# Normalizing on the eviction of spatial products taken by columns, full spectral products, high modes first, packed bias rows, scores without GpSimd

## The reference

```python
x = x + codano(group_norm(x))            # layer 0
t = t + attention(layer_norm(t)); t = t + experts(layer_norm(t))   # layer 1
# in codano, tn = instance_norm of each of 128 token images
k, q = fno_layer(tn, key...), fno_layer(tn, query...)    # to 64 x 64, 16 heads
v = fno_layer(tn, value...)                              # 128 x 128, 16 heads
p = softmax(q.k / scale)                                 # 32 x 32 for each head and batch
attn = fno_layer(p.v, proj...)                           # back to one channel
# fno_layer(x) = (conv1x1(x) + bias) + irfft(rfft(x)[low modes] * w)
```

## Time and profile before

| | us |
|---|---|
| runs of before, median of 3 (lowest, highest) | 2422.3 (2421.1, 2422.91) |
| the profiled execution, its own time | 2420.67 |
| its span | 2418.6 |
| stages tokens, modes, scores, mix (from the start of the span) | to 93.2, 123.2, 151.7, 248.8 |
| busy over the span: PE, DVE, ACT, POOL | 2090.5, 1936.0, 1710.9, 627.7 |

### The profile page before, as it was taken

One profiled execution on the slowest core, in us unless ns is written; L12 is line 12 of the kernel. 1 busy time (PEld: TensorE's weight loads), 2 busy tenths in 40 slices (PEclk: granted clock), 3 DMA queues, 4 the chain that ended last, 5 costly groups with the idle time before them and its releaser, 6 DMA issues. The chain is left out here.

```text
span 2418.6 us, 31035 instructions
## 1 busy us (share of the span) xinstructions
PE 2090.5 (86%) x10467; PEld 1065.6 (44%) x10467; DVE 1936.0 (80%) x3563; ACT 1710.9 (71%) x2429; POOL 627.7 (26%) x761
## 2 busy tenths in 40 slices
PE   8667548957499999999999999999999999766778
PEld 8522225743254444444444444444444444323333
DVE  4766888868788898898898888888888888767776
ACT  1454436639287888888888888888888888657776
POOL 0345403506501021022022022022000000036778
PEclk9888655556699999999999999999999999878999
DMA  9002443000000000000000000000000000000111
GB/s 301 1 35 105 114 108 76 1 0 1 6 1 1 1 1 1 1 1 1 1 1 1 1 1 1 1 1 1 1 1 1 1 1 1 9 14 23 31 32 44
DMA packets 80833, 55.72 MB, mean 23 GB/s; under 512 B 11283, under 2 KB 78739, under 8 KB 79140
## 3 DMA queue, kind: packets, MB, share of 16 engines
q1 hardware_dynamic: 75476, 52.38, 7.3%
q10 hardware_dynamic: 5200, 1.38, 0.3%
HBM read 36.90 MB, written 16.78 MB: 22 GB/s over the span
## 5 line engine op out<-in xcount | busy, mean ns | idle before, releaser
L1909 ACT ACTIVATE inner<-banks,key_bias,scales 128x1024 f32<-128x1024 f32 x512 | 616.9, 1205 | 211.6 <-PE banks L1782 205.9
L2031 DVE TENSOR_TENSOR weights_low<-weights,weights_high 128x1024 f16<-128x1024 f32 x512 | 674.7, 1318 | 17.0
L1916 ACT ACTIVATE weights<-inner 128x1024 f32<-128x1024 f32 x512 | 541.0, 1057 | 16.3 <-DVE weights_low L2031 0.3
L2027 DVE CAST weights_high<-weights 128x1024 f16<-128x1024 f32 x512 | 371.0, 725 | 181.5 <-ACT weights L1916 167.6
L2105 POOL CAST sums_high<-sums 128x512 f16<-128x512 f32 x32 | 39.1, 1222 | 1092.9 <-ACT sums L1899 1075.0
L1782 PE MATMUL banks<-queries_high,keys_high 128*128 128x512 f16 x1024 | 304.8, 379 | 0.7 <-ACT inner L1909 0.7
L1797 PE MATMUL banks<-weights_low,tokens_high 128*128 128x512 f16 x1024 | 304.8, 379 | 0.0
L1782 PE MATMUL banks<-queries_low,keys_high 128*128 128x512 f16 x1024 | 304.7, 379 | 0.0
L1797 PE MATMUL banks<-weights_high,tokens_low 128*128 128x512 f16 x1024 | 304.7, 379 | 0.0
L1797 PE MATMUL banks<-weights_high,tokens_high 128*128 128x512 f16 x1024 | 304.7, 379 | 0.0
L1782 PE MATMUL banks<-queries_high,keys_low 128*128 128x512 f16 x1024 | 304.7, 379 | 0.0
(11 more groups left out here) (592 smaller groups left out, 3373.7 us busy)
## 6 DMA issues: line engine op xcount, KB each, us to landing
images_b<-in_x SPq DMA_DIRECT2D x32, 256.0 KB, 9.1
images_a<-in_x SPq DMA_DIRECT2D x8, 1024.0 KB, 9.2
mixed_scratch<-images_a SPq DMA_DIRECT2D x4, 2048.0 KB, 6.3
result<-group_result SPq DMA_DIRECT2D x32, 256.0 KB, 2.3
images_b<-mixed_scratch SPq DMA_DIRECT2D x10, 768.0 KB, 5.1
...
```

The source lines that it names most:

```text
L1909: act.activation(m.inner[:, t % 2, :], m.pair[t % 2], ACT.Exp, scale=m.fs[:, 1:2], bias=m.kb[:, c // QN % 2, k:k + 1]).then_inc(s.inner, 1)
L1916: act.activation(m.wt[:, t % 2, :], m.inner[:, t % 2, :], ACT.Exp).then_inc(s.outer, 1)
L2027: vec.tensor_copy(m.wH[:, t % DEEP, :], m.wt[:, t % 2, :]).then_inc(s.high, 1)
L2031: vec.tensor_tensor(m.wL[:, t % DEEP, :], m.wt[:, t % 2, :], m.wH[:, t % DEEP, :], ALU.subtract)\
```

## The change

- Tokens: the parameters' transfers are issued first; VectorE makes the effective weights between the second and third quarter of its statistics; TensorE turns them and ScalarE evicts them ahead of the second transform; the averaging matmuls move from groups 29 and 31 to 26 and 28; a part of the statistics moves into the loop of low parts; there are five chunks.
- Modes: `m.hg` comes first on VectorE and TensorE, the low modes behind it; bias terms become three more rows (36 to 38) of the group `few`, by three further columns of the table `low`.
- Scores: VectorE makes j = 0, 1, 4 and half of the heads of 2, ScalarE the other half and 3; the eight bias matmuls are gone.
- Normalizing images_a in place is gone in three stages. A spatial product now takes the four columns of one group, so that its eviction can apply that group's scale and offset; the offset needs the row sums of the mixing matrix, one matmul and one VectorE instruction. `m.probT` is one full block-diagonal matrix, so that a spectral product is one matmul over 128 partitions, in a ring of three pairs of banks. All four stores wait for the last eviction.

```diff
 def stage_tokens(nc, held, m, ins, const):
-    chunks = [(0, 6), (6, 18), (18, 42), (42, 66)]
+    chunks = [(0, 6), (6, 18), (18, 36), (36, 54), (54, 66)]
...
-                    if g < len(SCALARS):
-                        scalar(g)
-                    elif g < len(SCALARS) + len(convs):
-                        conv(g - len(SCALARS))
-                    if g == 31:
+                    if g < len(convs):
+                        conv(g)
+                    elif g < len(convs) + len(SCALARS):
+                        scalar(g - len(convs))
+                    if g == 29:
                         act.wait_ge(s.added, 1)
+            act.wait_ge(s.wturned, 1)
+            act.copy(m.wT[:, 0:4].rearrange("p k c h -> p (k c h)"), m.ps[2])
+            act.copy(m.wT[0:MT[4][1], 4].rearrange("p c h -> p (c h)"), m.ps[3][0:MT[4][1], 0:128])
+            act.copy(m.wq[:, 0].rearrange("p c h -> p (c h)"), m.ps[3][:, 128:256])
+            act.copy(m.wq[0:FEW, 1].rearrange("p c h -> p (c h)"), m.ps[3][0:FEW, 256:384]).then_inc(s.wcopied, 1)
             act.wait_ge(s.fixed, 1)
...
-                if g == 29:
+                if g == 26:
...
-                if g == 31:
+                if g == 28:
...
-            pe.wait_ge(s.split, 3)
+            pe.wait_ge(s.split, 7)
+            pe.wait_ge(s.wready, 1)
+            pe.wait_ge(s.copied, NG)
+            for k, (m0, n) in enumerate(MT):
+                for cpt in (0, 1):
+                    o = m.ps[2][0:n, 64 * (2 * k + cpt):64 * (2 * k + cpt) + 64] if k < 4 else m.ps[3][0:n, 64 * cpt:64 * cpt + 64]
+                    pe.transpose(o, m.weff[:, cpt, m0:m0 + n], m.ident[0:64, 0:64])
+            for cpt in (0, 1):
+                pe.transpose(m.ps[3][:, 128 + 64 * cpt:192 + 64 * cpt], m.lowW[:, cpt], m.ident[0:64, 0:64])
+                mm = pe.transpose(m.ps[3][0:FEW, 256 + 64 * cpt:320 + 64 * cpt], m.fewW[:, cpt], m.ident[0:64, 0:64])
+            mm.then_inc(s.wturned, 1)
...
+                if q == 1:
+                    vec.wait_ge(s.weights, 16 * 8)
+                    vec.wait_ge(s.split, 7)
+                    effective_weights(vec, c, m, work[:, 1056:1072])
+                    vec.drain().then_inc(s.wready, 1)
...
-            vec.tensor_reduce(m.col[:, 6:7], inside, AX.X, ALU.add)
-            c.step(vec.tensor_reduce(m.col[:, 2:3], flat, AX.X, ALU.add))
-            c.step(vec.tensor_scalar(m.col[:, 2:3], m.col[:, 2:3], 1.0 / 256, None, ALU.mult))
...
+            vec.tensor_reduce(m.col[:, 6:7], inside, AX.X, ALU.add)
+            c.step(vec.tensor_reduce(m.col[:, 2:3], flat, AX.X, ALU.add))
+            c.step(vec.tensor_scalar(m.col[:, 2:3], m.col[:, 2:3], 1.0 / 256, None, ALU.mult))
+            low(0)
...
-            for g in range(8):
-                vec.tensor_scalar(m.a[:, :, g * 4:g * 4 + 4], m.a[:, :, g * 4:g * 4 + 4],
-                                  mean[:, g:g + 1], rstd[:, g:g + 1], ALU.subtract, ALU.mult)
...
+def effective_weights(vec, c, m, work):
+
+    weff = m.weff.rearrange("p c (r k) -> p c r k", r=ROWS)
+    wre, wim = weff[:, 0], weff[:, 1]
+    vec.tensor_copy(wre, m.wraw[:, :, :, 0])
+    c.step(vec.tensor_copy(wim, m.wraw[:, :, :, 1]))
+
...
+    c.step(vec.memset(wim[0:48, 0:1, 0], 0.0))
+    for cpt, half in ((0, wre), (1, wim)):
+        vec.tensor_copy(m.fewW[:, cpt, 0:36].rearrange("p (j i) -> p j i", j=4), over(half[:, 0:9, 0], 1, 4))
+        vec.tensor_copy(m.fewW[:, cpt, 36:FEW], half[:, 0, 0:1].to_broadcast([64, 3]))
+        pick = m.lowW[:, cpt].rearrange("p (a r k) -> p a r k", a=2, r=8)
+        vec.tensor_copy(pick[:, 0], half[:, 0:8, 1:9])
+        vec.tensor_copy(pick[:, 1], half[:, 18:26, 1:9])
 def stage_modes(nc, held, m):
...
-            vec.drain().then_inc(s.weights, 1)
+            h, f, by = m.hg.rearrange("p (x y) -> p x y", x=FQ), m.ft, m.col[:, 0:1]
+            c.step(vec.tensor_scalar(m.hg, m.ft.rearrange("p x y -> p (x y)"), by, 2.0, ALU.mult, ALU.mult))
...
+            c.step(vec.memset(h[:, :, 65:66], 0.0))
+            vec.drain().then_inc(s.high, 1)
+            c.step(vec.memset(m.fewX[:, :, 36:FEW], 1.0))
             form_modes(vec, c, m.ft, m.modes, K33)
...
             vec.drain().then_inc(s.modes, 1)
-
-            h, f, by = m.hg.rearrange("p (x y) -> p x y", x=FQ), m.ft, m.col[:, 0:1]
-            c.step(vec.tensor_scalar(m.hg, m.ft.rearrange("p x y -> p (x y)"), by, 2.0, ALU.mult, ALU.mult))
...
-            vec.drain().then_inc(s.high, 1)
-            vec.wait_ge(s.copied, len(banks))
...
+            bq, bk = m.biases[:, 0:16], m.biases[:, 16:32]
+            vec.tensor_tensor(m.pq[:, 0, 1], m.qk[:, 1, 16:32], bq, ALU.mult)
+            vec.tensor_tensor(m.pq[:, 1, 1], bq, bk, ALU.mult)
+            c.step(vec.tensor_tensor(m.pq[:, 3, 1], m.qk[:, 1, 0:16], bk, ALU.mult))
+            for i, j in ((0, 2), (1, 3), (3, 4)):
+                c.step(vec.scalar_tensor_tensor(out=m.aS, in0=m.pq[:, i, 1], scalar=m.low[:, j:j + 1], in1=m.aS,
+                                                op0=ALU.mult, op1=ALU.add))
...
-            c.step(vec.tensor_tensor(m.dck, over(m.modesT[0:1, 1, 1, :], 1, HEADS), over(w.r2[0:1], 2, P), ALU.mult))
-            c.step(vec.tensor_tensor(m.dck, m.dck, over(w.r3[0:1], 2, P), ALU.add))
...
         def _(pool):
-            for g in range(8, 16):
-                pool.tensor_scalar(m.a[:, :, g * 4:g * 4 + 4], m.a[:, :, g * 4:g * 4 + 4],
-                                   m.norms[1][:, g:g + 1], m.rstd[:, g:g + 1], ALU.subtract, ALU.mult)
...
-            for i, bank in enumerate(banks):
-                if i == 0:
-                    pe.wait_ge(s.weights, 1)
-                if bank[0][4] == 'modes':
-                    pe.wait_ge(s.modes, 1)
-                for j, (src, n, _, wide, _) in enumerate(bank):
-                    mm = pe.transpose(m.ps[i % NBK][0:n, j * P:j * P + wide], src, m.ident[0:wide, 0:wide])
-                mm.then_inc(s.turned, 1)
...
+            n = len(hbanks)
+            pe.wait_ge(s.modes, 1)
+            for u, (src, rows) in enumerate(((m.lowX, P), (m.fewX, FEW))):
+                reached(pe, s.copied, n + u - NBK + 1)
+                for cpt in (0, 1):
+                    mm = pe.transpose(m.ps[(n + u) % NBK][0:rows, cpt * P:cpt * P + P], src[:, cpt], m.ident)
                 mm.then_inc(s.turned, 1)
...
+            vec.tensor_tensor(m.few[0:FEW], over(m.modesT[0:FEW, 1, 0, :], 1, HEADS), over(m.aS[0:FEW], 2, P), ALU.mult)\
+                .then_inc(ready[4], 1)
+            x, a = operands(2, SPLIT)
+            vec.tensor_tensor(m.prod[:, 2, SPLIT:], x, a, ALU.mult).then_inc(ready[2], 1)
...
-                vec.tensor_copy(m.probT[q, :, NT * (b % 2):NT * (b % 2) + NT], m.probS[q])
+                vec.tensor_copy(m.probT[q, :, NT * b:NT * b + NT], m.probS[q])
...
-            x, a = operands(2)
-            pool.tensor_tensor(m.prod[:, 2], x, a, ALU.mult).then_inc(ready[2], 1)
-            pool.tensor_tensor(m.few[0:36], over(m.modesT[0:36, 1, 0, :], 1, HEADS), over(m.aS[0:36], 2, P), ALU.mult)\
-                .then_inc(ready[4], 1)
             pool.wait_ge(s.done, 1)
             pool.memset(m.probT, 0.0).then_inc(s.cleared, 1)
...
+            for h in range(SPLIT):
+                ins = act.activation(m.prod[:, 2, h, :], m.modesT[:, 0, 1, :], ACT.Copy, scale=m.aA[:, 0, h:h + 1])
+            ins.then_inc(ready[2], 1)
             for h in range(HEADS):
                 ins = act.activation(m.prod[:, 3, h, :], m.modesT[:, 0, 0, :], ACT.Copy, scale=m.aA[:, 2, h:h + 1])
             ins.then_inc(ready[3], 1)
-            for g in range(16, 32):
-                act.activation(m.a[:, :, g * 4:g * 4 + 4], m.a[:, :, g * 4:g * 4 + 4], ACT.Identity,
-                               bias=m.back[:, g:g + 1], scale=m.rstd[:, g:g + 1])
...
-            for i, j in enumerate((0, 2, 3, 1, 4)):
-                pe.wait_ge(ready[j], 1)
+            for j in (0, 1, 4, 2, 3):
+                pe.wait_ge(ready[j], 2 if j == 2 else 1)
...
-            for b in range(NB):
-                q = slice(NT * b, NT * b + NT)
-                pe.matmul(m.ps[0][q, :], m.modesT[0:1, 1, 1, q], m.dcq, start=False, stop=False)
-                mm = pe.matmul(m.ps[0][q, :], w.one[0:1], m.dck[:, :, q], start=False, stop=True)
...
 def stage_mix(nc, held, m, mix):
...
+            pe.matmul(m.ps[7][:, 0:1], m.mixA, m.unity[:, 0:1], start=True, stop=True).then_inc(s.summed_up, 1)
...
-                pe.matmul(m.ps[6 + n % 2], m.mixA, a[:, n * 512:n * 512 + 512], start=True, stop=True).then_inc(s.mixed, 1)
+                if n == 1:
+                    pe.wait_ge(s.offset, 1)
+                pe.matmul(m.ps[6 + n % 2], m.mixA, m.a[:, :, 4 * n:4 * n + 4], start=True, stop=True).then_inc(s.mixed, 1)
...
-                for part in (1, 0):
-                    if part:
-                        reached(pe, s.used, i - 1)
-                    else:
-                        reached(pe, s.odd, i)
```

(35 more changed lines are left out.)

173 lines of the change are left out of this document (73 added, 100 removed).

## The result

The changed kernel took 2404.27 us (median of 5 runs, 2400.02 to 2409.21), the kernel before, run beside it, 2421.1 us (5 runs, 2419.55 to 2422.91). The ratio is 0.9932, with a 95% interval of 0.9916 to 0.9949: 16.8 us faster. The forecast was 2411.5 with a range from 2406: the direction held, and the gain was half as large again as the forecast one, just outside the range.

The account below looks back on a forecast made before the run. No engine was busy throughout, so the wait ending last in each of four stages was taken as the bound; -1.5 (tokens) - 7.4 (modes) - 4.9 (scores) + 3.0 (mix) = -10.8 us gave 2411.5 us, range 2406 to 2419.

Parts of the forecast that it names:

- the price in mix: Mix: each spectral product becomes one full matmul, 1.06 instead of 0.64 us; a step 4.24 instead of 3.38; stage +3.0.
- The stall: Mix: during VectorE's reduction, the eviction that TensorE wants comes 0.45 us late, counted three times.
- the 5.3 us of work that needs nobody: Mix: TensorE's work behind the last product VectorE takes before its reduction (4.46 us), letting TensorE go on meanwhile.
- no fall of the clock: Mix: TensorE's clock would not drop after the reductions; no time counted for slower matmuls.
- Modes: Stage modes: hg comes first and the Gram matrix ends last, 22.3 us for 29.7; -7.4 us (-6 to -9).
- next in line, by 0.7: Modes: VectorE's own path, 20.4 us, ends 0.7 us ahead of the Gram matrix's end at 21.1.
- the forecast's remark on GpSimd's normalizing: Modes: the better end of -6 to -9 us if this work, now gone, had stretched VectorE's small rows.
- Scores: Stage scores: without GpSimd's reads beside them, VectorE products take 2.28 us instead of 5.68; -4.9 us (-3 to -6).
- Tokens: Stage tokens: last group 0.7 us later, high parts 1.0 earlier, one round done early; -1.5 us (+0.5 to -3).
- Strided operand: Rival, mix: the spatial product's operand in 16-byte runs is slow; doubling the product adds 34 us, 2445; chance 0.05.
- Products slow by themselves: Rival, scores: VectorE products stay at 5.68 us, +6.7 in place of -4.9, 2423 us; chance 0.09.
- Clock and order: Rival: lower clock and idling after mix's reductions, lower clock in scores, stores ending mix; +8.5, 2420 us; chance 0.1.

Follow-up runs that it names:

- before_again: The kernel before, unchanged, profiled once more to see how its stages vary between executions: 2418.17 us (one run).
- gpsimd_reads: The changed kernel, but in stage scores GpSimd makes product group 2 again instead of VectorE and ScalarE: 2407.52 us (one run).

## Why the prediction missed its range

**The step that failed** is the price in mix: "one matmul of 128 rows and 512 columns, the spatial one's shape: 1.06 instead of 0.64 us. A step costs TensorE 4 x 1.06 = 4.24". The 1.06 is right for a full matmul between row-tiled ones, which is where stage mix of the kernel before had it. It is 0.86 behind another full one, and the 0.64 held 0.2 of the same kind: among their own kind it is 0.86 against 0.43, a factor of 2.0 and not 1.7. One row of the kernel before could have warned. In its last steps no spatial product stands between the two spectral ones:

```profile
230.01 1.08 PE L910 MATMUL banks<-images_b,modes 64*66 64x256 f32 x8 [0.71 <-ACT images_b L935]
```

One product's row lasts 0.70 us, so two at 0.64 would last 1.34. They last 1.08.

The change gave up row tiling and with it four changes of kind a step, so that a step went from 3.38 to 3.43 us, not to 4.24. In numbers, to the last eviction (forecast 76.2 us into the stage, measured 208.20 - 137.73 = 70.5): 16 steps 54.9 for 67.8, -12.9; stalls 3 x 1.94 for 3 x 0.45, +4.5; slow matmuls at a lower clock, forecast as none, +3.8 (2.77, 3.12, 2.12, 1.82 and 2.56 us from start to start for 1.72); start and last eviction -1.1. Sum -5.7. The stall was forecast too small, in part by the same error: the 5.3 us of work that needs nobody are 4.3 at 0.86 a matmul, an estimate that gives 1.0 of the missing 1.5 us. The slow matmuls behind it were a term put at nothing, "no fall of the clock". Right was that the stall would persist, and where. The fourth reduction came at 75.9 for 81.5, and what follows it is unchanged (18.7 us). The stores ended 3 us ahead of the stage, as worked out.

**Modes** (-7.4, measured -8.48): the order as forecast, and the Gram matrix is what ends last. VectorE's path, "next in line, by 0.7", ended 2.9 us ahead: it was 3.3 us shorter than the sum's 20.4, as the forecast's remark on GpSimd's normalizing allowed. The size was off by the clock: the turning of hg took 5.45 us for the earlier trace rows's 6.40 (granted clock 0.72 for 0.59), but before_again has 5.45 too, and a stage of 28.75. Over the seven executions with this code the stage took 21.2 to 22.5, 7.3 us less on average than the two of before.

**Scores** (-4.9, measured -5.56): products of 2.25 us as forecast, for the reason weighed and then confirmed. The end of the scores came 9.8 us into the stage for 10.6, with the last groups at clock 1.00 in this execution. With the lower clock there the stage is 25.4 us and the gain 3.1; the term's range of -3 to -6 held both.

**Tokens** (-1.5, measured +0.06) was wrong: the last group came 2.5 us later, not 0.7. The cost of the averaging matmuls was taken as 0.7 for about 1.3, "the transfers that ScalarE issues earlier lie in its idle time" looked at ScalarE alone and not at the loads beside them, and the profiled execution has the earliest end (93.6) of seven that reached up to 98.6. Their mean is 95.8, 2.2 us behind the kernel before and outside the term's range, so +0.06 is luck. The turning stood in the sum with 2.85 us (1.55 and 1.3); taken off the path it gave 1.8.

**The rivals.** Strided operand: out, 0.86 us. Products slow by themselves: out, by gpsimd_reads. Clock and order: the stalls and slow matmuls that it named came, 9.6 us of them, and were more than paid by the step.
